# A graph-attention layer on one core: units fetched in single rows every 9 chunks in place of 11, with 40 of the 128 rows issued by ScalarE in place of 24

## The reference, cut to what matters

```
n_in  = node[recv]                  # [E, 128]
n_out = node[send]                  # [E, 128], a gather of 206250 rows
wn    = n_out @ W_lin + b_lin
e     = leaky_relu(concat(n_in, n_out) @ W_att + b_att, 0.2)
a     = e @ w_alpha                 # one number for each edge
alpha = softmax of a over the edges of one receiver
n_i   = segment_sum(alpha * wn, recv)
x     = layernorm(x + elu(n_i))
```

## Time and profile before

| | |
|---|---|
| median of three runs | 2260.75 us |
| the profiled execution | 2259.84 us, of which 2258.1 us from the first to the last instruction (the span) |
| busy in the span: PE, PEld | 1811.7 us, 1421.1 us |
| busy in the span: DVE, ACT, POOL | 1855.0 us, 1468.1 us, 1582.8 us |
| granted TensorE clock, mean | 0.961 of full speed |
| DMA | 293.30 MB, 130 GB/s |

### The profile page before, as it was taken

The page is one execution under the profiler, slowest core; times in us unless marked ns, Lnnn a source line. Parts: engine busy times, 40 slices in busy tenths (PEclk is TensorE's granted clock), DMA queues, the critical chain, the costliest instruction groups (busy, mean ns, idle before and its releaser), DMA issues.

```text
span 2258.1 us, 63519 instructions
## 1 busy us (share of the span) xinstructions
PE 1811.7 (80%) x11705; PEld 1421.1 (63%) x11705; DVE 1855.0 (82%) x5630; ACT 1468.1 (65%) x4913; POOL 1582.8 (70%) x1658
## 2 busy tenths in 40 slices
PE   5648888888988888887888988888889878888870
PEld 2336666666766776666666767666667666666660
DVE  9849988888789889887998998888776667676667
ACT  2326677777666776665666776666666666666665
POOL 2057777777777777777777777777777777777760
PEclk9769999999999999999999999999999999999995
DMA  3134444445444444444444445444454544444431
GB/s 122 56 112 139 136 137 134 135 134 142 131 135 134 135 137 133 136 138 130 135 136 131 130 138 137 138 134 136 133 137 136 138 137 134 138 135 136 136 109 57
DMA packets 168219, 293.30 MB, mean 130 GB/s; under 512 B 41346, under 2 KB 112894, under 8 KB 167825
## 3 DMA queue, kind: packets, MB, share of 16 engines
q0 software_dynamic: 78288, 213.62, 33.2%
q1 hardware_dynamic: 87029, 74.44, 12.1%
q10 hardware_dynamic: 2508, 1.18, 0.2%
HBM read 278.10 MB, written 10.99 MB: 128 GB/s over the span
## 4 chain that ended last, share of the span: by engine, by line
POOL 17%; issue 12%; DVE 9%; PE 8%; DMA 3%; ACT 2%; DVEq 2%; ACTq 1%; POOLq 0%
POOL rows L666 17%; DMA rows<-qv_table,senders 3%; DVE sums L1625 2%; PE turned_ps L1033 2%; PE hidden_ps L1007 2%; DVE leaky L1581 2%; PE masked_ps L1018 2%; DVEq L1625 1%; PE hidden_ps L1005 1%; PE turned_ps L1025 1%; DVEq L443 1%; ACT spare L778 1%; ACTq L810 1%; DVE keys L1186 1%; DVE keys L1185 1%
## 5 line engine op out<-in xcount | busy, mean ns | idle before, releaser
L666 POOL DMA_INDIRECT rows<-qv_table,senders x1623 | 1555.1, 958 | 496.3 <-issue 468.0
L1033 PEld LDWEIGHTS turned_ps<-rows,spare 128*128 128x128 f32 x3246 | 423.2, 191 | 479.7 <-ACT spare L793 368.6
L1625 DVE SCALAR_TENSOR_TENSOR sums<-sums,shrink,turned_ps 128x129 f32 x1660 | 573.2, 345 | 135.8 <-PE turned_ps L1033 59.4
L778 ACT ACTIVATE spare<-masked_ps,peaks 128x128 f32<-128x128 f32 x1660 | 472.0, 368 | 303.6 <-DVE peaks L1603 225.3
L1033 PE MATMUL turned_ps<-rows,spare 128*128 128x129 f32 x3246 | 501.6, 287 | 173.7 <-ACT spare L793 91.2
L1007 PE MATMUL hidden_ps<-onehotT,p_unit 128*128 128x128 f32 x3320 | 591.2, 280 | 0.0
L1005 PE MATMUL hidden_ps<-identf,rows 128*128 128x128 f32 x1623 | 454.6, 280 | 143.9 <-DMA rows<-qv_table,senders 132.9
L1007 PEld LDWEIGHTS hidden_ps<-onehotT,p_unit 128*128 128x128 f32 x3320 | 519.3, 197 | 0.6 <-issue 0.6
L761 ACT ACTIVATE p_unit<-p_all 128x128 f32 x1660 | 410.4, 316 | 106.3 <-issue 83.1
L1588 DVE TENSOR_REDUCE lows<-masked_ps 128x4 f32<-128x512 f32 x415 | 285.2, 687 | 192.5 <-PE masked_ps L1018 191.4
L1018 PE MATMUL masked_ps<-leaky,w_cols 128*128 128x512 f32 x830 | 426.6, 595 | 0.0
(11 more groups left out here) (203 smaller groups left out, 920.3 us busy)
## 6 DMA issues: line engine op xcount, KB each, us to landing
single_rows<-qv_table SPq DMA_DIRECT2D x3848, 1.0 KB
lanes_all<-lane_list SPq DMA_DIRECT2D x415, 128.0 KB
rows<-qv_table,senders POOLq DMA_INDIRECT x1623
single_rows<-qv_table ACTq DMA_DIRECT2D x888, 1.0 KB
qv_table<-rows SPq DMA_DIRECT2D x24, 256.0 KB, 2.2
out<-x_sb SPq DMA_DIRECT2D x1, 1344.0 KB
out<-x_sb SPq DMA_DIRECT2D x1, 896.0 KB
kept<-windows SPq DMA_DIRECT2D x3, 208.0 KB
```

Source lines behind the costliest of these rows:

```text
L666: g.indirect_dma_start(out=rows[:, k % U, c, 0:R], out_offset=None, in_=table, in_offset=bass.IndirectOffsetOnAxis(ap=senders[:, s % 2, c ...
L778: last = a.activation(weightsT[:, k % 2, unit], masked_ps[:, k % 2, unit], ACT.Exp, bias=peaks[:, at + 2 * n:at + 2 * n + 1])
L1033: mm = t.matmul(unit_sums_ps[:, c, :], weights[:, k % 2, c * P:(c + 1) * P], rows_at_unit(k, c)[:, F:PLACE], start=True, stop=True)
L1625: v.scalar_tensor_tensor(out=at, in0=at, scalar=shrink[:, k % 4, i:i + 1], in1=unit_sums_ps[:, i, :], op0=ALU.mult, op1=ALU.add).then_inc( ...
```

## The change

Two constants change. The rest follows from them.

```
-    ROW_CHUNKS = 11
-    BY_ACT = 3 * ROWS_EACH
+    ROW_CHUNKS = 9
+    BY_ACT = 5 * ROWS_EACH
     BY_SP = UNIT - BY_ACT
     ROWS_TO = [BY_SP * n // ROW_CHUNKS for n in range(ROW_CHUNKS + 1)]
     ACT_ROWS_TO = [BY_SP + BY_ACT * n // ROW_CHUNKS for n in range(ROW_CHUNKS + 1)]
```

## The result

The changed kernel takes 2368.22 us, median of six runs (2363.62 to 2371.84). The kernel before took 2260.89 us on the same chip, also in six (2259.41 to 2263.27). The ratio is 1.0473 [1.0462, 1.0483]: slower by 107 us, where 58 had been forecast. The profiled execution took 2366.05 us, with a span of 2364.3 us. TensorE's mean granted clock is 0.959 against 0.961 before and has no part in this.

The account below looks back on a forecast made before the run. POOL's gathers were taken to bound the kernel, with consumers merely keeping up before 902 us. From 2259.84 us, 11.3 came off for gathers and 69 were added for ACT's felt issuing: 2318 us, range 2262 to 2440.

Parts of the forecast that it names:

- the forecast's own: Whole kernel: a share of 0.41 to 0.72 of ACT's added issuing is felt, 2274 to 2364 us; chance 0.5.
- everything felt, or nearly: Rival outcome for the whole kernel: nearly all of ACT's added issuing is felt, over 2364 us; chance 0.17.
- ACT's slack: ACT's waits at L768 and L787 together, 33.2, 31.8 and 94.8 us by stretch, subtracted from the felt issuing.
- the three stretches: Parts of the loop before the change: 178 to 902 us (146 chunks), 902 to 1351 (90), from 1351 (171).
- The 11.3 us of POOL: On POOL: 9 gathers fewer at 1.25 us each, taken off the time as a gain.
- The share of 0.6: On ACT: the part of the added issuing that a chunk feels, 0.56 us a chunk; ends 0.41 and 0.72.
- the added 0.94 us a chunk: ACT's sequencer: 952 row DMAs more at 0.32 us and 119 loads more at 0.73 us, 392 us in all.
- SP at nothing: SP's 200 added rows and 506 loads for 481 cost nothing: 4.56 us a chunk against 4.86.
- The ring and the prologue at nothing: POOL's eight-chunk buffer ring (3 us left) and ACT's added issuing at the start (5.6 us) cancel; ends -3 and +6 us.
- POOL stays the bound: Rival: ACT's added issuing is done beside queued activations, so only the 9 gathers count; 2248.6 us, chance 0.11.
- Everything is felt: Rival: ACT's sequencer never gets ahead, all 0.94 us a chunk less slack counts; 2471 us; with nearly-everything, chance 0.17.
- only the counted chunks: Rival: only the 49 counted chunks of the first stretch feel ACT's added issuing; 2284 us; up to no change, chance 0.17.

Follow-up runs that it names:

- the best placement: Changed kernel with ACT's address loads moved right behind `weigh` and its row DMAs between `copy_weights` and `lessen`; 2252.76 us.
- the loads that went with their rows: Changed kernel with ACT's rows issued only for the first two units, all loads meant to stay; trace has 10 loads, not 230; 2250.05 us.

## Why the prediction was right, and where its sizes were off

**The direction and the mechanism were right.** ACT's sequencer time holds up `weigh`, PE gets its weights late, the ring fills up and POOL waits. The signs named for this are there: 1.25 us a gather where POOL isn't held, 130.6 us of waits for PE (100.2 of them before 1400 us), a longer idle time ahead of L778, a shorter wait at L768 in the last stretch, and loaded chunks longer than others with the same rows. A chunk of the first stretch takes 797 / 146 = 5.46 us, where 5.3 had been named. One sign failed: at L787 the wait in the last stretch stays at 6.0 us. Rows don't land late: in the 46 chunks with single rows PE is idle for 0.3 us in all ahead of L1005. The result lies in the range, but 4 us above the forecast's own (2274 to 2364). By its time alone it falls to what the prediction called everything felt, or nearly, with a chance of 0.17; the shares below are what speaks for the forecast's own account.

**Two terms were off in how the parts were put together, and a third in its size.**

*ACT's slack can't all be spent.* ACT by lines, L768 and L787 in the three stretches of the kernel after, to be set beside the earlier trace rows:

```profile
L768 ACT ACTIVATE sloped<-hidden_ps 128x512 f32<-128x512 f32 x146 | 89.3, 612 | 9.0 <-PE hidden_ps L1007 9.0
L787 ACT ACTIVATE shrink<-growth 128x4 f32<-128x4 f32 x146 | 33.8, 231 | 8.7 <-DVE growth L1613 8.5
...
L768 ACT ACTIVATE sloped<-hidden_ps 128x512 f32<-128x512 f32 x90 | 55.2, 613 | 5.8 <-PE hidden_ps L1007 5.7
L787 ACT ACTIVATE shrink<-growth 128x4 f32<-128x4 f32 x90 | 20.6, 229 | 9.1 <-DVE growth L1613 9.1
...
L768 ACT ACTIVATE sloped<-hidden_ps 128x512 f32<-128x512 f32 x171 | 104.8, 613 | 6.1 <-PE hidden_ps L1007 5.9
L787 ACT ACTIVATE shrink<-growth 128x4 f32<-128x4 f32 x171 | 40.1, 234 | 6.0 <-DVE growth L1613 5.9
```

By stretches 17.7, 14.9 and 12.1 us are left unspent, 45 us of the 160 that I had taken off. Waits of single chunks don't add up to an account that other chunks may draw on.

*The 11.3 us of POOL weren't to be had.* I took them off although the sum said that the consumers set the pace. Only one of the two can hold in a stretch. They show where POOL is the bound, as without ACT's rows.

These two, 45 + 11, cover the 49 us that were missing (107 - 58), and 7 more: 4 lie in the felt part of the issuing, below, and 2 outside the three stretches.

*A load between rows costs more than 0.73 us.* Of the 230 loads, 92 stand ahead of their group of rows. A group of four then takes 2.18 us in place of 1.45, and the 0.73 is right. The other 138 stand between rows, and there four rows with a load take 2.52 to 2.58 us, 1.1 us more. So from the first to the last of these sequencer instructions a chunk's issuing takes 2.10 us in place of 1.05. The change adds 1.05 us a chunk and not 0.94: 434 us in all in place of 392, so 42 us were left out.

**The share of 0.6 came out, but in part by luck.** Growth of a stretch plus slack spent, over the added 0.94 us a chunk: (73 + 15.5) / 137 = 0.65, (32 + 16.9) / 85 = 0.58, (4 + 82.7) / 161 = 0.54. Over the 1.05 us that the issuing really grew by, the shares are 0.58, 0.52 and 0.48: more was issued than I had counted, a smaller part of it was felt, and the two errors nearly cancel. A mean also hides who pays. The row view that I read it from had said it: the load was felt in full, the third row not at all. In the changed kernel the chunks without a load stay under POOL's pace on average and those with one go over it, and without 184 of the loads 83 us come back.

**The other terms.** SP at nothing held, with about a third of the cover I had named. The ring and the prologue at nothing held too: POOL's last gather ends 106.5 us later, and its first starts 1.4 us earlier.

**The rivals.** *POOL stays the bound* is what the kernel would do with the same issuing in another place: I had 2248.6 us for it, and the best placement takes 2252.76. The page "Advanced Engine Details and Errata" of the Trainium skill, section "Sequencer Loop", says that engine instructions can be queued while the sequencer executes a control instruction. The trace agrees as far as work ahead of the DMA in the program goes (L793 at 856.72 us starts beside a row DMA), and behind `stage_p` there is too little of it. Of work behind the DMA the kernel after shows no such case: none of its 415 `weigh` starts while a row is being issued. *Everything is felt* (2471 us) and *only the counted chunks* (2284 us) are out by the windows.

## What to carry to other kernels

In this kernel the sequencer work of a computing engine, register loads and DMA issues, had a price where no earlier activation was left to run beside it and where the instruction behind it was one that PE soon needed. So put it behind activations that are already released and ahead of an instruction with slack, keep each chunk's portion shorter than that cover, and keep loads out of a group of row DMAs. Don't subtract a gain at one engine and a loss at another in the same stretch, since only the later of them sets the pace. Where an idle time ends right behind a DMA issue on the same engine, look at the sequencer first, whatever releaser is named. And an edit can take away more than was meant, as with the loads that went with their rows: the counts in the trace tell it.

## What was not expected of the hardware

In these traces the length of a load of eight addresses on ACT goes with how soon it follows a row DMA. In the kernel after the 138 loads that come within 0.1 us of a row have a median of 839 ns, and nearly all others, over 2 us behind one, 575 ns. The overall median of 764 ns only mixes the two. The other orders agree: 582 ns with one load a unit, ahead of its rows, 575 ns behind `weigh` with the rows at L793, and 736 ns behind `weigh` with the rows at the end of the step, where most loads come 0.1 to 0.5 us behind the last row. Why is open. Also a row on ACT takes 0.23 us behind another row, but 0.46 us as the first of a group or behind a load, so a load in the midst of a group costs twice.

The same 40 rows and 5 loads a unit, moved about within one chunk of ACT's order, gave times from 2252.76 to 2385.79 us, a range of 133 us with no computation changed. The page "DMA: Bandwidth & Descriptors" of the Trainium skill, section "Issuing engines are not separate DMA queues", calls the time to start a DMA usually small beside the transfer. No run here sets a row's issue against its transfer, but starting the rows on ACT behind `stage_p`, with their address loads, cost 120 us of the program's 2368.
